# Where VectorE adds the next turn's rows in two attention stages of a four-layer kernel

## The chip, the cores and the metric

The kernel runs on one core of a Trainium2 chip, as one program. The metric is device time in microseconds, here the median of three runs. A core has TensorE (PE in the rows; its weight loads PEld), VectorE (DVE), ScalarE (ACT), GpSimd (POOL) and SyncE (SP), each with a program of its own that it runs in order; semaphores tie them together. DMA queues move data between HBM and SBUF.

## The reference

Four layers, each an attention and a mixture-of-experts feed-forward, with a residual sum after each; x is 32 x 128 x 128 in f32. What matters here is the second attention and the fourth, and the sum ahead of each:

```python
x = x + _L0_ffn_ref(_layernorm(x), ...)
x = x + _L1_xattn_ref(_layernorm(x), ctx_1024, ...)
...
x = x + _L2_ffn_ref(_layernorm(x), ...)
x = x + _L3_xattn_ref(_layernorm(x), ctx_1024, ctx_1024, mask, ...)
```

A feed-forward gives each token two experts' rows; the token's x becomes x + w0·row0 + w1·row1. The second attention is linear: q is a softmax over 8 channels of each of 16 heads, multiplied with a small matrix per batch entry, normed, added to q and projected. The fourth is an ordinary masked softmax attention with one head.

## The kernel before, in words

Tokens are held in SBUF as 32 tiles of 128 x 128, in eight groups of four. An attention runs in two turns (`TURNS` = 2); a turn works on four groups side by side, called streams w = 0 to 3 (`W` = 4), each with two PSUM banks of its own.

In both stages the program of VectorE for turn i is:

- `head_norms` (L481): scales, then the normed rows of all four streams (L477); TensorE waits for them.
- A `weave` (L94) of generators. It calls each once per round, in order, until all have ended. Four are the streams' `body`, the fifth is `next_rows` (L487), which prepares the rows of turn i + 1.
- `tail_norms`, the aggregates, scales and norms for the router of the next feed-forward; then `tail_dve` (L555), the top experts from the router's logits.

In the second attention `body` (L1679) has three steps: the maxima of the query heads and the subtraction (L1673, L1674), the head step (L1686 to L1693), and the sum into x with its statistics (L1696, L460). In the fourth, `body` (L2481) has: the maxima of the scores (L2484, L2485), the reciprocals (L2488), the final sum into x (L2493).

For one stream `next_rows` waits until the loaded pair of expert rows is there, adds it into x with eight instructions (`combine`, L523), and takes statistics and aggregates (L460, L456): four of each. These sixteen instructions are called a block here; block w is that of stream w. The tuple `rounds` says how many blocks go into each call of the generator. With (2, 2), blocks 0 and 1 follow the first step of all four bodies, blocks 2 and 3 the second step. Only turn 0 has a next turn, so turn 1 runs without blocks.

The pairs are loaded by SP at the start of the stage, in eight transfers of 512 KB (`load_pairs`, L1562), four for turn 0 and four for turn 1. In the fourth attention GpSimd scatters the rows to their experts (L2408) as soon as VectorE knows the places, and SP loads expert weights behind the pairs.

Of the kernel before, what the change touches and what calls it, by code (L numbers as in the profile page):

```python
# [4 lines left out]


# [1 line left out]

# [85 lines left out]
def weave(bodies):  # L94


    bodies = list(bodies)
    while bodies:
        bodies = [b for b in bodies if next(b, "end") != "end"]
# [14 lines left out]
def build(nc, A, out):  # L114
    with ExitStack() as top:
# [70 lines left out]
        W = 4  # L186
# [300 lines left out]
        def next_rows(dve, ch, i, st, here, rounds):  # L487

            if i < TURNS:
                w = 0  # L490
                for n in rounds:
                    for _ in range(n):
                        here(i, w)
                        known(dve, ch, st, w, x_tile(i * W + w))
                        w += 1
                    yield
                assert w == W
# [1133 lines left out]
        def attention_1(layer_before):  # L1631
            assert layer_before in SCATTERED
            with ExitStack() as ph:
                SS = streams(pe=["turn_u", "q", "turn_q", "out", "turn_o", "proj"],
                             act=["u_turned", "q_exp", "q_turned", "o_turned"],
                             dve=["u_normed", "q_less", "o"])
# [23 lines left out]
                @block.vector  # L1660
                def _(dve):
                    ch = Chain(dve)

                    def heads(ap):
                        return ap.rearrange("p (h c) -> p h c", c=8)

                    def wide(ap):
                        return ap.unsqueeze(2).to_broadcast([P, G * 16, 8])

                    def less_max(t, name, rows):  # L1670

                        red = t["red"][:, 0, :].rearrange("p (j h) -> p j h", h=16)
                        ch.link(dve.tensor_reduce(red, rows, AX.X, ALU.max))  # L1673
                        return dve.tensor_tensor(t[name].rearrange("p (j h c) -> p j h c", h=16, c=8), rows, red.unsqueeze(3).to_broadcast([P, G, 16, 8]), ALU.subtract)  # L1674

                    def here(i, w):
                        combine_stream(dve, ch, i, w, layer_before)

                    def body(w, i, S, t):  # L1679
                        g, A_, B_ = i * W + w, t["A"], t["B"]  # L1680
                        dve.wait_ge(S.pe.sem, S.PE.at(i, "q"))
                        less_max(t, "q", A_.rearrange("p (j h c) -> p j h c", h=16, c=8)).then_inc(S.dve.sem, S.DVE.tick("q_less"))
                        yield
                        dve.wait_ge(S.pe.sem, S.PE.at(i, "out"))
                        three = A_[:, 0:3 * KX].rearrange("p (j c) -> p j c", c=KX)
                        dve.reciprocal(t["dinv"][:, 0:3, :], three[:, :, P:KX])  # L1686
                        ch.link(dve.reciprocal(t["dinv"][:, 3, :], B_[:, P:KX]))
                        o, q = flat(t["u"][:, :, :]), t["q"].rearrange("p (j h c) -> p j h c", h=16, c=8)
                        dve.tensor_tensor(t["u"][:, 0:3, :].rearrange("p j (h c) -> p j h c", c=8), three[:, :, 0:P].rearrange("p j (h c) -> p j h c", c=8),
                                          t["dinv"][:, 0:3, 0:16].unsqueeze(3).to_broadcast([P, 3, 16, 8]), ALU.mult)  # L1690
                        dve.tensor_tensor(heads(t["u"][:, 3, :]), heads(B_[:, 0:P]), t["dinv"][:, 3, 0:16].unsqueeze(2).to_broadcast([P, 16, 8]), ALU.mult)
                        ch.link(dve.tensor_tensor(q, q, t["dinv"][:, :, 16:32].unsqueeze(3).to_broadcast([P, G, 16, 8]), ALU.mult))
                        dve.tensor_tensor(o, o, t["q"], ALU.add).then_inc(S.dve.sem, S.DVE.tick("o"))  # L1693
                        yield
                        dve.wait_ge(S.pe.sem, S.PE.at(i, "proj"))
                        ch.link(dve.tensor_tensor(flat(group(X, g)), flat(group(X, g)), A_[:, :], ALU.add))  # L1696
                        stats_of(dve, st_tail, w, x_tile(g))
                        yield
                    for _ in next_rows(dve, ch, 0, st, here, (W,)):
                        pass  # L1700
                    ch.link()
                    for i in range(TURNS):
                        head_norms(dve, ch, i, SS, st, T)
                        weave([body(w, i, SS[w], T[w]) for w in range(W)] + [next_rows(dve, ch, i + 1, st, here, (2, 2))])
                        ch.link()
                        tail_norms(dve, ch, i, SS, st_tail, T, taken=True)
                        weave(tail_dve(dve, ch, i * W + w, i, SS[w], T[w]["tl"], T[w]["A"]) for w in range(W))

                @block.scalar
# [655 lines left out]
        def attention_3(layer_before):  # L2365
            SCALE = float(P) ** -0.5
            with ExitStack() as ph:
# [109 lines left out]
                @block.vector  # L2477
                def _(dve):
                    ch = Chain(dve)

                    def body(w, i, S, t):  # L2481
                        g, A_ = i * W + w, t["A"]
                        dve.wait_ge(S.pe.sem, S.PE.at(i, "scores"))
                        ch.link(dve.tensor_reduce(t["nmax"][:, :], A_[:, :].rearrange("p (j l) -> p j l", j=G), AX.X, ALU.max, negate=True))  # L2484
                        dve.tensor_scalar(t["nmax"][:, :], t["nmax"][:, :], SCALE, None, ALU.mult).then_inc(S.dve.sem, S.DVE.tick("max"))  # L2485
                        yield
                        dve.wait_ge(S.act.sem, S.ACT.at(i, "exp"))
                        ch.link(dve.reciprocal(t["rinv"][:, :], t["sums"][:, :]))  # L2488
                        yield
                        dve.wait_ge(S.pe.sem, S.PE.at(i, "mixed"))  # L2490
                        for j in range(G):
                            xt = x_tile(g)(j)
                            dve.scalar_tensor_tensor(xt, A_[:, j * P:(j + 1) * P], t["rinv"][:, j:j + 1], xt, ALU.mult, ALU.add)  # L2493
                        yield
                    ch.link(dve.tensor_scalar(region[:, :], iota8[:, :], float(REGION), None, ALU.mult))
                    dve.tensor_copy(ends[:, :], region[:, :])

                    def placed(i, w):
                        own, B_ = slice(w * G, (w + 1) * G), T[w]["B"]
                        dve.wait_ge(places_made.sem, NG + i * W + w + 1)  # L2500
                        ch.link(dve.tensor_tensor(place[:, own, :], B_[:, 0:G * E].rearrange("p (j e) -> p j e", e=E), ends[:, :].unsqueeze(1).to_broadcast([P, G, E]), ALU.add))
                        dve.tensor_tensor(ends[:, :], ends[:, :], B_[:, G * E:(G + 1) * E], ALU.add)
                        ch.link(dve.tensor_tensor(place[:, own, :], place[:, own, :], hot[:, own, :], ALU.mult))
                        ch.link(dve.tensor_reduce(spot_f[:, own], place[:, own, :], AX.X, ALU.add))
                        dve.tensor_copy(spots[:, i, own], spot_f[:, own]).then_inc(positions_made.sem, 1)

                    def here(i, w):
                        combine_stream(dve, ch, i, w, layer_before)
                    for _ in next_rows(dve, ch, 0, st, here, (W,)):
                        pass  # L2510
                    for i in range(TURNS):
                        head_norms(dve, ch, i, SS, st, T)
                        weave([body(w, i, SS[w], T[w]) for w in range(W)] + [next_rows(dve, ch, i + 1, st, here, (2, 2))])
                        ch.link()
                        tail_norms(dve, ch, i, SS, st_tail, T)
                        for w in range(W):
                            weave([tail_dve(dve, ch, i * W + w, i, SS[w], T[w]["tl"], T[w]["A"], [hot])])
                            if w:
                                placed(i, w - 1)
                        placed(i, W - 1)  # L2520
                    ch.link()
                    dve.tensor_copy(pad_at, ends[0:1, :]).then_inc(ends_known.sem, 1)
                    tile_tables(dve, ch, TILES_TOP1, ends[:, :], region[:, :], marks, scratch)
                    dve.tensor_tensor(expo, LG[:, :, :], MX[:, :, 0:1].to_broadcast([P, B, E]), ALU.subtract).then_inc(leads_made.sem, 1)
                    dve.wait_ge(leads_exp.sem, 2)
                    ch.link(dve.tensor_reduce(scratch[:, 7, 0:B], expo, AX.X, ALU.add))
                    dve.reciprocal(WT[:, 0, :], scratch[:, 7, 0:B])
# [33 lines left out]
```

## Time and profile before

| What | us |
|---|---|
| median of three runs | 1773.26 |
| lowest, highest | 1766.41, 1776.73 |
| span of the profiled execution (first to last instruction) | 1780.2 |
| TensorE busy | 1444.8 (81%) |
| VectorE busy | 1162.8 (65%) |
| ScalarE busy | 818.9 (46%) |
| GpSimd busy | 764.0 (43%) |
| mean granted clock of TensorE | 0.880 |

For the profiled execution the record gives its span alone, so its own time stands here as 1780.2 us from the first to the last instruction, with nothing known to lie around it. Busy shares are averages over stages with different limits, so the stages have to be read one by one. The second attention lies between about 380 and 530 us of the span, the fourth between 1518 and 1650.

### The profile page before, as it was taken

To read this page: it belongs to the slowest core of one execution; us is meant where nothing else is said; L and a number is where in the kernel's file an instruction comes from. 1 tells how busy PE (TensorE), PEld (TensorE's weight loads), DVE (VectorE), ACT (ScalarE), POOL (GpSimd) and SP (SyncE) were. 2 spreads that over 40 slices of the span, in tenths; PEclk is the share of its full clock that TensorE was granted. 3 is DMA by queue.
4 is the path that set the end of the run, shared out by engine and by line. 5 is a ranking of instruction groups with operands and counts; after the bars stand their busy time and mean duration, and the time that the engine had idled before them with its cause. 6 is when DMAs were issued, how large, how long until landed. Compare 5 with 4: busy or idle time off the path is not lost. (4 is left out here: it accounts for less than half of the span.)

```text
span 1780.2 us, 37318 instructions
## 1 busy us (share of the span) xinstructions
PE 1444.8 (81%) x10610; PEld 1313.5 (74%) x10611; DVE 1162.8 (65%) x3689; ACT 818.9 (46%) x2528; POOL 764.0 (43%) x757
## 2 busy tenths in 40 slices
PE   6686699927767489999999999999997698446494
PEld 4565499925556389999999999999996698235494
DVE  5657744448675467778787777878785565585343
ACT  4252255512212166666666666666663233314252
POOL 3137344410003454546556565647463466012442
PEclk9696899966667699999999999999998799767697
DMA  9101122230121300000000000000000232500224
GB/s 236 21 19 58 48 59 62 62 111 1 48 94 49 118 13 1 13 1 18 9 17 7 15 9 13 10 0 12 1 13 13 76 84 76 189 12 15 73 64 120
DMA packets 94154, 82.79 MB, mean 47 GB/s; under 512 B 17076, under 2 KB 81047, under 8 KB 93927
## 3 DMA queue, kind: packets, MB, share of 16 engines
q1 hardware_dynamic: 74952, 52.24, 10.6%
q0 software_dynamic: 11936, 24.55, 4.2%
q10 hardware_dynamic: 7168, 4.86, 1.0%
q8 instruction: 42, 0.69, 0.2%
q14 instruction: 56, 0.46, 0.1%
HBM read 51.93 MB, written 31.25 MB: 47 GB/s over the span
## 5 line engine op out<-in xcount | busy, mean ns | idle before, releaser
L1980 POOL TENSOR_TENSOR paired_rows<-paired_rows,rinv 128x1024 f32<-128x1024 f32 x128 | 242.3, 1893 | 288.3 <-DVE rinv L2263 284.8
L2254 DVE TENSOR_TENSOR probs_turned_lo<-psum_banks,probs_turned_hi 128x512 fp32r<-128x512 f32 x256 | 175.6, 686 | 99.7 <-ACT probs_turned_hi L2128 92.9
L2146 ACT ACTIVATE paired_rows<-psum_banks,neg_max 128x256 f32<-128x256 f32 x512 | 237.4, 490 | 0.2
L2027 PE MATMUL psum_banks<-y_turned_parts,queries_hi 128*128 128x256 f32 x1024 | 201.4, 294 | 3.0 <-DVEq L1881 3.0
L2062 PE MATMUL psum_banks<-probs_turned_hi,y_rows 128*128 128x512 f32 x512 | 191.8, 415 | 0.4 <-issue 0.4
L2128 ACT CAST probs_turned_hi<-psum_banks 128x512 fp32r<-128x512 f32 x256 | 151.1, 590 | 56.8 <-PE psum_banks L2011 54.3
L2268 DVE TENSOR_REDUCE neg_max<-psum_banks 128x4 f32<-128x1024 f32 x128 | 156.4, 1222 | 8.9 <-PE psum_banks L2027 4.7
L2027 PEld LDWEIGHTS psum_banks<-y_turned_parts,queries_hi 128*128 128x128 f32 x1024 | 159.2, 192 | 3.6 <-issue 3.6
L2011 PE MATMUL psum_banks<-ident,paired_rows 128*128 128x128 f32 x1024 | 154.7, 274 | 7.7 <-DVEq L1881 4.4
L2128 ACT CAST queries_hi<-psum_banks 128x512 fp32r<-128x512 f32 x128 | 75.0, 586 | 174.7 <-PE psum_banks L2050 168.3
L2027 PE MATMUL psum_banks<-y_turned_parts,queries_lo 128*128 128x256 f32 x512 | 145.3, 284 | 0.0
L2074 PEld LDWEIGHTS psum_banks<-expert_w_a,paired_rows 128*128 128x128 f32 x1024 | 133.8, 191 | 11.9 <-DVE paired_rows L2278 0.7
L2050 PE MATMUL psum_banks<-expert_w_b,expert_w_a 128*128 (+1 forms) x1024 | 139.0, 279 | 2.8 <-ACT tail_turned L2118 1.8
L2074 PE MATMUL psum_banks<-expert_w_a,paired_rows 128*128 128x128 f32 x1024 | 134.8, 274 | 0.5 <-issue 0.5
L2050 PEld LDWEIGHTS psum_banks<-expert_w_b,expert_w_a 128*128 128x128 f32 x1024 | 126.5, 194 | 6.3 <-ACT tail_turned L2118 3.2
L2011 PEld LDWEIGHTS psum_banks<-ident,paired_rows 128*128 128x128 f32 x1024 | 119.8, 142 | 10.3 <-DVEq L1881 5.1
L2254 DVE TENSOR_TENSOR queries_lo<-psum_banks,queries_hi 128x512 fp32r<-128x512 f32 x128 | 88.5, 692 | 42.3 <-ACT queries_hi L2128 35.8
L1410 POOL DMA_INDIRECT expert_rows<-expert_rows_sb,tile_rows x71 | 70.6, 994 | 103.1 <-DVE expert_rows_sb L1497 103.1
L1470 ACT ACTIVATE hidden<-psum_banks,tile_w 128x128 f32<-128x128 f32 x284 | 81.2, 368 | 71.0 <-PE psum_banks L1436 71.0
L2146 ACT ACTIVATION_READ_ACCUMULATOR paired_rows<-psum_banks,neg_max 128x1 f32 x512 | 113.4, 221 | 0.0
L2062 PEld LDWEIGHTS psum_banks<-probs_turned_hi,y_rows 128*128 128x128 f32 x512 | 96.4, 188 | 17.1 <-issue 0.5
L2062 PE MATMUL psum_banks<-probs_turned_lo,y_rows 128*128 128x512 f32 x256 | 100.8, 394 | 0.0
(691 smaller groups left out, 3330.1 us busy)
## 6 DMA issues: line engine op xcount, KB each, us to landing
paired_rows<-expert_rows SPq DMA_DIRECT2D x16, 512.0 KB, 6.0
tile_rows<-rows_by_expert SPq DMA_DIRECT2D x110, 64.5 KB
tile_rows<-rows_by_expert_first SPq DMA_DIRECT2D x71, 64.5 KB
expert_w_b<-in_L_ffn_w_dram SPq DMA_DIRECT2D x2, 2048.0 KB, 12.7
tile_rows<-expert_rows SPq DMA_DIRECT2D x8, 512.0 KB, 3.6
x_rows<-in_x_dram SPq DMA_DIRECT2D x8, 256.0 KB, 5.3
normed_rows_dram<-paired_rows SPq DMA_DIRECT2D x1, 2048.0 KB, 8.7
expert_w_a<-in_L_ffn_gate_up_w_dram SPq DMA_DIRECT2D x1, 2048.0 KB, 9.5
```

The lines of the kernel that those rows point to most:

```text
L1410: pool.indirect_dma_start(ys, bass.IndirectOffsetOnAxis(ap=to, axis=0), yo[:, i % SLOTS, :], None).then_inc(expert_out[i % SLOTS].sem, 16)
L1470: ins = act.activation(hidT[:, s % 2, c * P:(c + 1) * P], hidden_bank(s, c // 2)[:, c % 2 * P:(c % 2 + 1) * P], ACT.Gelu, bias=w1[:, s % 4 ...
L1980: ins = pool.tensor_tensor(probs[:, p, :, :], probs[:, p, :, :], rinv[:, p, :].unsqueeze(2).to_broadcast([P, 4, 256]), ALU.mult)
L2011: ins = pe.transpose(bank[T_BANK][:, h * P:(h + 1) * P], probs[:, par, h, c * P:(c + 1) * P], ident[:, :])
L2027: ins = pe.matmul(bank[S_BANKS[par] + h // 2][:, (h % 2) * 256:(h % 2 + 1) * 256], queries[q][:, h, :], yparts[:, 2 * s2 + y, :], start=(k ...
L2050: ins = pe.matmul(bank[Q_BANK][:, h * P:(h + 1) * P], wqk[:, 4 * u3 + h, :], flat(KVT[:, bass.ds(b3, 1), P:2 * P]), start=True, stop=True)
L2062: ins = pe.matmul(bank[Z_BANK][:, :], yrows[:, 2 * s1 + y, k * P:(k + 1) * P], probsT[p][:, (u + 1) % 2, k, :], start=(k == 0 and n == 0), ...
L2074: ins = pe.matmul(bank[Y_BANK][:, 0:P], mixed[:, par, h, :], wvo[:, 4 * u0 + h, :], start=(u0 == 0 and h == 0), stop=(u0 == 3 and h == 3), ...
L2128: ins = act.copy(dst, bank[bank_][:, :])
L2146: ins = act.activation(probs[:, par, h, :], bank[S_BANKS[par] + h // 2][:, (h % 2) * 256:(h % 2 + 1) * 256], ACT.Exp, bias=nmax[:, par, h: ...
L2254: ins = dve.tensor_tensor(lo, bank[bank_][:, :], hi.bitcast(F32), ALU.subtract)
L2268: ins = dve.tensor_reduce(nmax[:, par, :], ps[:, S_BANKS[par]:S_BANKS[par] + 2, :].rearrange("p r (h k) -> p (r h) k", k=256), AX.X, ALU.m ...
```

## The change

In both stages the generator `next_rows` is made before the weave and called once ahead of it. In the second attention its rounds become (1, 1, 1, 0, 1): block 0 comes between `head_norms` and the maxima, block 1 behind the maxima, block 2 behind the head step, none behind the sums, and block 3 between `tail_norms` and `tail_dve`. `itertools.islice(ahead, 3)` lets the weave take just three calls. In the fourth attention the rounds stay (2, 2): blocks 0 and 1 come between `head_norms` and the maxima, blocks 2 and 3 behind the maxima.

```diff
@@ second attention
                     for i in range(TURNS):
                         head_norms(dve, ch, i, SS, st, T)
-                        weave([body(w, i, SS[w], T[w]) for w in range(W)] + [next_rows(dve, ch, i + 1, st, here, (2, 2))])
+                        ahead = next_rows(dve, ch, i + 1, st, here, (1, 1, 1, 0, 1))
+                        next(ahead, None)
+                        weave([body(w, i, SS[w], T[w]) for w in range(W)] + [itertools.islice(ahead, 3)])
                         ch.link()
                         tail_norms(dve, ch, i, SS, st_tail, T, taken=True)
+                        for _ in ahead:
+                            pass
                         weave(tail_dve(dve, ch, i * W + w, i, SS[w], T[w]["tl"], T[w]["A"]) for w in range(W))
@@ fourth attention
                     for i in range(TURNS):
                         head_norms(dve, ch, i, SS, st, T)
-                        weave([body(w, i, SS[w], T[w]) for w in range(W)] + [next_rows(dve, ch, i + 1, st, here, (2, 2))])
+                        ahead = next_rows(dve, ch, i + 1, st, here, (2, 2))
+                        next(ahead, None)
+                        weave([body(w, i, SS[w], T[w]) for w in range(W)] + [ahead])
                         ch.link()
                         tail_norms(dve, ch, i, SS, st_tail, T)
```

## Rows read from the trace of the kernel before

**Rows 1.** Windows: us, busy of PE, PEld, DVE, ACT, POOL; clock, DMA, GB/s.

```profile
380.00:530.00 150.00, 89.68 (x432) 71.44 (x432) 108.22 (x474) 28.92 (x57) 0.34 (x1) 0.61 0.19 64
...
640.00:1480.00 840.00, 808.57 (x6241) 765.34 (x6240) 629.79 (x1447) 496.89 (x1545) 473.53 (x436) 0.98 0.06 18
...
1518.00:1650.00 132.00, 71.13 (x392) 50.65 (x392) 91.22 (x506) 41.79 (x121) 20.34 (x21) 0.71 0.23 74
```

**Rows 2.** Timeline of VectorE, second attention, turn 0: start, us, instruction, idle before it.

```profile
408.19 0.69 DVE L1673 TENSOR_REDUCE head_sums<-psum_banks 128x64 f32<-128x512 f32 x1 [3.75 <-PE psum_banks L1743]
...
417.19 2.35 DVE L523 SCALAR_TENSOR_TENSOR x_rows<-paired_rows,mix_weights,x_rows 128x128 f32<-128x128 f32 x8
...
420.85 2.32 DVE L523 SCALAR_TENSOR_TENSOR x_rows<-paired_rows,mix_weights,x_rows 128x128 f32<-128x128 f32 x8
...
424.48 0.73 DVE L1686 RECIPROCAL d_inv<-psum_banks 128x96 f32<-128x96 f32 x1
...
436.76 2.35 DVE L523 SCALAR_TENSOR_TENSOR x_rows<-paired_rows,mix_weights,x_rows 128x128 f32<-128x128 f32 x8
...
444.06 0.65 DVE L1696 TENSOR_TENSOR x_rows<-x_rows,psum_banks 128x512 f32<-128x512 f32 x1
...
450.33 1.17 DVE L456 BATCH_NORM_AGGREGATE mean_var___<-norm_stats___ 128x2 f32<-128x6 f32 x16
...
459.71 0.19 DVE L557 COPY tail_logits____<-psum_banks 128x32 f32<-128x32 f32 x1 [2.44 <-PE psum_banks L588]
```

**Rows 3.** Timeline of VectorE, second attention, turn 1, which has no blocks.

```profile
488.01 0.76 DVE L1686 RECIPROCAL d_inv<-psum_banks 128x96 f32<-128x96 f32 x1 [2.58 <-PE psum_banks L1762]
...
504.14 0.69 DVE L1696 TENSOR_TENSOR x_rows<-x_rows,psum_banks 128x512 f32<-128x512 f32 x1 [3.75 <-PE psum_banks L1743]
...
506.66 0.69 DVE L1696 TENSOR_TENSOR x_rows<-x_rows,psum_banks 128x512 f32<-128x512 f32 x1 [0.89 <-PE psum_banks L1743]
...
511.44 1.17 DVE L456 BATCH_NORM_AGGREGATE mean_var___<-norm_stats___ 128x2 f32<-128x6 f32 x16
...
521.58 0.19 DVE L557 COPY tail_logits____<-psum_banks 128x32 f32<-128x32 f32 x1 [3.21 <-PE psum_banks L588]
```

**Rows 4.** Timeline of VectorE, fourth attention, turn 0.

```profile
1550.62 0.69 DVE L2484 TENSOR_REDUCE neg_max<-psum_banks 128x4 f32<-128x512 f32 x1 [7.65 <-PE psum_banks L2427]
...
1554.15 2.35 DVE L523 SCALAR_TENSOR_TENSOR x_rows<-paired_rows,mix_weights,x_rows 128x128 f32<-128x128 f32 x8
...
1562.42 2.35 DVE L523 SCALAR_TENSOR_TENSOR x_rows<-paired_rows,mix_weights,x_rows 128x128 f32<-128x128 f32 x8
...
1569.72 1.09 DVE L2493 SCALAR_TENSOR_TENSOR x_rows<-psum_banks,rinv,x_rows 128x128 f32<-128x128 f32 x4
1570.73 1.12 DVE L2493 SCALAR_TENSOR_TENSOR x_rows<-psum_banks,rinv_,x_rows 128x128 f32<-128x128 f32 x4
```

**Rows 5.** Timeline of VectorE, fourth attention, turn 1, which has no blocks.

```profile
1614.45 0.17 DVE L2485 TENSOR_SCALAR neg_max___<-neg_max___ 128x4 f32<-128x4 f32 x1
...
1619.44 1.13 DVE L2493 SCALAR_TENSOR_TENSOR x_rows<-psum_banks,rinv,x_rows 128x128 f32<-128x128 f32 x4 [1.56 <-PE psum_banks L2435]
```

**Rows 6.** Timelines of TensorE (second and fourth attention, turn 0) and GpSimd.

```profile
438.48 2.08 PE L1743 MATMUL psum_banks<-wsmall,u_turned 128*128 128x128 f32 x8
...
445.66 1.16 PE L1743 MATMUL psum_banks<-wsmall,u_turned___ 128*128 128x128 f32 x8
...
1557.90 5.38 PE L2435 MATMUL psum_banks<-ctx_rows,expert_w_a 128*128 x32
...
1643.80 0.96 POOL L2408 DMA_INDIRECT rows_by_expert<-paired_rows,top_experts  x1 [32.13 <-DVE top_experts L2505]
```

**Rows 7.** Timeline of SP's issues of the pair loads, and all landings on that tile.

```profile
378.81 10.01 SPq L1562 DMA_DIRECT2D paired_rows<-expert_rows  x8
...
1518.68 8.69 SPq L1562 DMA_DIRECT2D paired_rows<-expert_rows  x8
...
DMA to landing us min/median/max: 1.6/6.2/12.2
```

More of the change, by code:

```diff
@@ L7 @@
 from contextlib import ExitStack
+import itertools
 import concourse.bass as bass
```

## The prediction

> **What bounds the kernel now.** I began with busy time by stage. In the second attention (380 to 530 us) and the fourth (1518 to 1650) no engine is full: VectorE works 108.2 of 150 and 91.2 of 132 us, TensorE 89.7 and 71.1 at a granted clock of 0.61 and 0.71, DMA moves little [rows 1]. Such a stage is bound by a chain that hops between engines, so I next read VectorE in order of time, with the idle time before each row and what ended it. VectorE runs its program in order, so the rows of the next turn (eight adds, four statistics and four aggregates for each of four streams) stand between other steps and push them back, unless they lie where VectorE would have waited anyway. Turn 1 of each attention has no next turn: it shows the same chain without them, and so how long each wait really is [rows 3, 5].
>
> One such block takes half of the way from 417.19 to 424.48, 3.645 us [rows 2]. Four make 14.58 us in each attention. In turn 0 of the second attention VectorE waits 3.75 us before the first maximum and 2.44 before the first logits, with no block in either; in the fourth it waits 7.65 us before its first maximum while four blocks stand behind the maxima [rows 2, 4]. Those waits are what can be used.
>
> **The change, part by part.** No instruction is added or removed. In the second attention blocks 0 and 3 move, 32 instructions of VectorE with their drains (blocks 1 and 2 keep their places); in the fourth all four blocks do, 64. No DMA, no SP or GpSimd instruction moves; each block takes its wait for its pair of rows along.
>
> Second attention, turn 0:
>
> (a) Block 0 goes ahead of the maxima. VectorE is free at 408.19 − 3.75 = 404.44; the block runs to 408.09. The first projection is there at 408.19 [rows 2]. Cost nothing, with 0.10 us to spare; without that cover it would be 3.65.
>
> (b) Block 1 alone now stands behind the maxima, 417.19 to 420.84. Would the products be there? In turn 1 VectorE waits 2.58 us at this point [rows 3], which gives 419.8 here. So the block decides, and the head step starts at 420.84 and not at 424.48: 3.64 earlier.
>
> (c) The head step takes 436.76 − 424.48 = 12.28 us [rows 2], to 433.12. Block 2 runs to 436.76. The projection comes 3.75 us behind the head step by turn 1 [rows 3], at 436.87. The sums thus start at 436.87 for 444.06: 7.19 earlier, and now a wait of TensorE decides.
>
> (d) The sums and statistics took 450.33 − 444.06 = 6.27 us because the projections of all streams had long been there. With the projection just in time, turn 1 shows 511.44 − 504.14 = 7.30, a wait of 0.89 in it [rows 2, 3]. I take 7.30, since the cover is gone as in turn 1: aggregates at 444.17, 6.16 earlier.
>
> (e) Scales and norms take 459.71 − 2.44 − 450.33 = 6.94 us, to 451.11; block 3 runs to 454.76. The first logits come 9.38 us (turn 0) or 10.14 (turn 1) behind the aggregates, by 453.55 or 454.31 [rows 2, 3]. The block ends last: the tail starts at 454.76 for 459.71. Gain 4.95 us. Nothing waits for block 3 before the norms of turn 1, which stand behind the tail.
>
> Bounds: 1.03 more if the projections are there in time after all (step d), so 6.0; below, turn 1's pace of logits would cost up to a microsecond in the tail and a late first maximum some tenths, so 3.9. I keep 4.95, the sum by the nearest rows.
>
> Fourth attention, turn 0:
>
> (f) Blocks 0 and 1 go ahead of the maxima: VectorE is free at 1550.62 − 7.65 = 1542.97, two blocks end at 1550.26, scores come at 1550.62 [rows 4]. Nothing exposed, 0.36 to spare; without cover 7.29.
>
> (g) Blocks 2 and 3 take the place of 0 and 1 behind the maxima. The reciprocals follow as before and end at 1562.42, where the third block used to start. The final step then starts there and not at 1569.72 [rows 4]: 7.30 earlier. Is its input there? In turn 1 it comes 1619.44 − 1614.62 = 4.82 us after the last maximum [rows 5], here at about 1559.1. TensorE's 32 products end at 1563.28 [rows 6], and VectorE reaches the fourth stream only at 1562.42 + 3 x 1.01 = 1565.5. So nothing waits. What is late next is VectorE itself: 3.3 us of blocks stay exposed. Bounds: 7.30 above, since only that much leaves the path; 6.4 below, if the wait for logits behind it grows by the 0.9 us by which it differs between turns of the second attention (2.44 and 3.21) [rows 2, 3].
>
> **Rows must have landed.** VectorE now wants turn 1's first rows at 404.44 and 1542.97. SP has issued all eight loads by 388.82 and 1527.37, and the slowest landing is 12.2 us after its issue [rows 7]: 401.0 and 1539.6. No wait.
>
> **Does the gain reach the end?** Behind both attentions each step follows on the one before: the row scatter of the fourth starts at 1643.80 after GpSimd sat idle 32 us [rows 6], so it moves with VectorE. The weights loads in these stages are issued after steps of the same chain. Nothing in the rows is tied to an absolute time. Sum: 4.95 + 7.30 = 12.25 us, 0.69% of the profiled span of 1780.2. That span is 7 us above the median of 1773.26, so the profiled execution was one of the longer ones; the two stages hold no row that would account for it, so I take the same 12.25 off the median: 1761.0.
>
> **TensorE's clock.** In this stage the granted clock is 0.61, a mix of the two levels, 1.2 and 2.4 GHz. Eight projection matmuls take 2.08 us at the low level, soon after TensorE stood idle, and 1.16 at the high one [rows 6]. The change shortens idle times of TensorE in turn 0, so the level may rise earlier or later in each burst. The blocks hide most of it: only step (d) would gain, by 1.03 us, giving 1760.0. The Trainium skill (TensorE: Matmul & The Clock Gate, HAM oscillation) says that bursts parted by waits start at the low clock each time; by that rule, which the first projection row bears out, step (d) stays at 7.30.
>
> **The rivals.** (A) Forecast, chance 0.64: 10.3 to 13.3 us by the bounds, 1761.0; with the scatter of medians (the three runs shown span 10.3 us) 1756 to 1767.
> (B) One attention keeps its time, 0.20: in the second the chain is tight at (a) and (c), by 0.10 and 0.11 us, and a delay of the first maximum could run through; then the time is 1773.26 − 7.30 = 1766.0, within 0.5% of before. For it: spare of a tenth only. Against: the second to fourth maximum each have a wait of their own ahead, which absorbs some.
> (C) The moved adds change nothing, 0.08: the weave could put the blocks in the same places, or another engine ends last, so 1773. Against: VectorE's idle rows name TensorE's outputs, and these wait for VectorE in turn.
> (D) The gain passes, but TensorE gets its clock at other points in later stages. The stretch 640 to 1480 holds TensorE busy for 808.6 of 840 us at 0.98 [rows 1]. If its granted clock fell to 0.966, 1.5% of 840 us would be 12.3 us and eat the gain; from 0.955 on (2.5%, 21 us) the kernel is slower by over 0.5%, about 1782. For it: the stretch is entered 5 us earlier, in another phase. Against: at this busy share the rows show 0.98 and no sign of a fall. 0.04.
> (E) The rows of turn 1 come late, against the landing above: VectorE would hold the first maximum, and each microsecond of lateness costs one. 0.04, about 1768.
>
> **How the numbers follow.** What this kernel's measurement can tell from no change is about 0.5%, 8.9 us. Of case A some 0.05 falls short of it by scatter, and 0.03 of B fall beyond it: 0.64 - 0.05 + 0.03 = 0.62 faster. Slower is D, 0.04, and 0.01 of C by scatter: 0.05. The rest is within: 0.33. The range has to take in A and B with the scatter, and leaves C, D and some of E out: 1754 to 1770.
>
> **What would show it.** The profile after should have: block 0 at 404.4 and the first maximum of the second attention still 3.75 us behind the norms; three further blocks, behind the maxima, the head step and the norms; sums with a wait of TensorE before them; the tail some 50.3 us behind the norms of turn 0 (before 55.3). In the fourth: two blocks in the former 7.65 us wait, the final step 19.4 us behind the norms (before 26.7). A DMA wait before a moved block, a maximum later than 408.5, or a clock under 0.97 between the two attentions would prove it wrong.

## The result, and the profile after

The changed kernel takes 1772.48 us, median of nine runs (1762.07 to 1778.21). The kernel before, run nine times with it, takes 1781.72 (1766.41 to 1788.1). The ratio is 0.9943 with a 95% interval of 0.992 to 0.9965: 10.2 us faster (the two medians stand 9.24 apart). That is 0.57%, just beyond the 0.5% named as what can be told from no change. The forecast ratio, 1761.0 / 1773.26 = 0.9931, lies inside the interval; the forecast time, 1761.0 with a range up to 1770, does not hold 1772.48. Three executions of 2523 to 4906 us, in the two kernels with block 0 back and with two blocks ahead, are in no ratio below.

Timeline of VectorE in the second attention of the changed kernel, turn 0 (start, us, instruction, idle before it and what ended it). Lines stand one to five higher than before:

```profile
408.76 1.11 DVE L478 TENSOR_SCALAR u_rows___<-x_rows,mean_var__,rstd__ 128x128 f32<-128x128 f32 x4
409.79 1.14 DVE L524 SCALAR_TENSOR_TENSOR x_rows<-paired_rows,mix_weights,x_rows 128x128 f32<-128x128 f32 x4
411.36 1.14 DVE L524 SCALAR_TENSOR_TENSOR x_rows<-paired_rows,mix_weights,x_rows 128x128 f32<-128x128 f32 x4 [0.44 <-issue]
...
413.82 0.66 DVE L1674 TENSOR_REDUCE head_sums<-psum_banks 128x64 f32<-128x512 f32 x1
...
416.16 0.69 DVE L1674 TENSOR_REDUCE head_sums_<-psum_banks 128x64 f32<-128x512 f32 x1 [0.92 <-PE psum_banks L1748]
...
422.62 2.35 DVE L524 SCALAR_TENSOR_TENSOR x_rows<-paired_rows,mix_weights,x_rows 128x128 f32<-128x128 f32 x8
...
426.28 0.72 DVE L1687 RECIPROCAL d_inv<-psum_banks 128x96 f32<-128x96 f32 x1
...
438.55 2.35 DVE L524 SCALAR_TENSOR_TENSOR x_rows<-paired_rows,mix_weights,x_rows 128x128 f32<-128x128 f32 x8
...
442.38 0.69 DVE L1697 TENSOR_TENSOR x_rows<-x_rows,psum_banks 128x512 f32<-128x512 f32 x1
...
444.92 0.69 DVE L1697 TENSOR_TENSOR x_rows<-x_rows,psum_banks 128x512 f32<-128x512 f32 x1 [0.91 <-PE psum_banks L1748]
...
447.33 0.69 DVE L1697 TENSOR_TENSOR x_rows<-x_rows,psum_banks 128x512 f32<-128x512 f32 x1 [0.77 <-PE psum_banks L1748]
...
450.57 1.26 DVE L457 BATCH_NORM_AGGREGATE mean_var___<-norm_stats___ 128x2 f32<-128x6 f32 x16
...
457.52 2.34 DVE L524 SCALAR_TENSOR_TENSOR x_rows<-paired_rows,mix_weights,x_rows 128x128 f32<-128x128 f32 x8
...
461.18 0.16 DVE L558 COPY tail_logits____<-psum_banks 128x32 f32<-128x32 f32 x1
```

The stage begins 5.43 us later in this profile than in that of before, which has nothing to do with the change; take 5.43 off to compare with [rows 2]. Block 0 stands in the former wait of 3.75 us. It needs 4.03 us and not 3.64, as VectorE had no next instruction for 0.44 us in its middle, so the first maximum is 0.2 us late, where the forecast had 0.1 to spare; the second still waits 0.92 for TensorE, and block 1 starts at 417.19 on the old clock, to the hundredth where it stood. Head step at 420.85 (forecast 420.84), block 2, sums at 436.95 (436.87). Then the sums have two waits for TensorE, 0.91 and 0.77, where the forecast had one of 0.89: they take 8.19 us, not 7.30. Block 3 stands behind the norms and the logits wait for it: tail at 455.75 (forecast 454.76, before 459.71).

The fourth attention, turn 0, same view:

```profile
1541.39 2.36 DVE L524 SCALAR_TENSOR_TENSOR x_rows<-paired_rows,mix_weights,x_rows 128x128 f32<-128x128 f32 x8
...
1549.16 0.69 DVE L2489 TENSOR_REDUCE neg_max<-psum_banks 128x4 f32<-128x512 f32 x1 [0.38 <-PE psum_banks L2432]
...
1552.68 2.35 DVE L524 SCALAR_TENSOR_TENSOR x_rows<-paired_rows,mix_weights,x_rows 128x128 f32<-128x128 f32 x8
...
1560.95 1.12 DVE L2498 SCALAR_TENSOR_TENSOR x_rows<-psum_banks,rinv,x_rows 128x128 f32<-128x128 f32 x4
...
1577.72 0.19 DVE L558 COPY tail_logits________<-psum_banks 128x32 f32<-128x32 f32 x1 [2.06 <-PE psum_banks L589]
```

Two blocks lie in the wait and leave 0.38 us of it (forecast 0.36). The final step has no wait before it and starts 1560.95 − 1541.39 = 19.56 us behind the norms (forecast 19.4, before 26.7).

From here on a stage's length is the time from the first scale row (`newton<-mean_var`) of turn 0 to that of turn 1. It was 68.16 us in the second and 60.44 in the fourth attention, and is 64.80 and 53.46: 3.36 and 6.98 shorter, 10.34 together. Windows of the changed kernel over the two stages and the long stretch between them (columns as in [rows 1]) show the granted clock of that stretch unmoved:

```profile
380.00:535.00 155.00, 93.45 (x442) 75.48 (x443) 110.91 (x485) 30.82 (x59) 2.24 (x2) 0.60 0.20 66
640.00:1480.00 840.00, 808.64 (x6247) 766.00 (x6247) 629.68 (x1448) 496.08 (x1543) 473.30 (x435) 0.98 0.07 18
1517.00:1641.00 124.00, 70.27 (x392) 50.13 (x392) 91.00 (x505) 41.84 (x121) 20.27 (x21) 0.73 0.25 79
```

The spans of the two profiles differ by less than the stages, 1780.2 and 1772.4: the second attention begins 5.4 us later in the profile of the changed kernel, the way from it to the fourth takes 3.6 us less (1066.79 for 1070.38), and what follows the fourth 0.7 more. All three lie outside the change; where this scatter comes from is taken up below.

### The profile page after: what moved, and what is told of

It reads as the page before. It is cut to its first block and busy times, and to the rows that moved or that the text cites. A ratio compares the mean times of both kernels' runs of the same rounds, so it can differ in the third digit from the quotient of the medians.

```text
span 1772.4 us, 37318 instructions
## 1 busy us (share of the span) xinstructions
PE 1439.5 (81%) x10610; PEld 1307.8 (74%) x10611; DVE 1164.0 (66%) x3689; ACT 819.1 (46%) x2528; POOL 764.3 (43%) x757
## 3 DMA queue, kind: packets, MB, share of 16 engines
q1 hardware_dynamic: 74952, 52.24, 11.2%
```

## The experiments

Open after the result: whether the two stage gains reach the end, what a block costs in each place, and why the absolute time missed by 11 us where the ratio fits. Ratios are to the kernel before, run on the same chip beside each group.

**The changed kernel, once more.** No edit.

> The changed kernel once more, beside before on the same chip, to separate the gain from the scatter of the time. Theory 1 (the stage gains of the profile after, 3.4 us in the second attention and 7.0 in the fourth, reach the end and nothing else changes): 10.3 us faster, ratio 0.9942. Rival (the forecast sum of 12.25 holds on average and the first profile of after was one with slow projections in the second attention): ratio 0.9931, and in this profile the sums of the second attention, turn 0, take 7.3 us and not 8.2. Rival (part of the gain is lost behind the stages): ratio above 0.996.

Measured: 0.9919 (0.9895 to 0.9943), 1763.4 us beside 1777.91. Stages 61.85 and 53.25. The sums took 8.30 us, so the forecast's 7.30 is not what turn 0 shows. This ratio alone would fit the forecast sum; the next repeats decide.

**One attention at a time.** The other one has its line of before:

```diff
-                        ahead = next_rows(dve, ch, i + 1, st, here, (2, 2))
-                        next(ahead, None)
-                        weave([body(w, i, SS[w], T[w]) for w in range(W)] + [ahead])
+                        weave([body(w, i, SS[w], T[w]) for w in range(W)] + [next_rows(dve, ch, i + 1, st, here, (2, 2))])
```

> Only the second attention has the new places; the fourth is as before. Theory 1: the time from the norms of turn 0 to those of turn 1 falls from 68.15 to 63.3 - 65 us, 3.4 us faster in all, ratio 0.9981. Forecast's sum: 4.95 us, 0.9972. Rival (a late first maximum runs through): no gain, 1.000.

> Only the fourth attention has the new places; the second is as before. Theory 1: 7.0 us faster, ratio 0.9961, and with the run above the two gains add up to that of both. Rival (the two interfere through the point at which TensorE's clock rises): the sum of the two differs from both together by over 3 us.

Measured: second alone 0.9973 (0.9951 to 0.9996), fourth alone 0.998 (0.9966 to 0.9994). The fourth's stage is 53.12, its full 7 us shorter, yet the time fell by 3.6 only. And the second attention of the kernel with only the fourth changed, whose code there is that of before, took 63.27 us and not 68.16. Its rows on TensorE, turn 0:

```profile
404.06 0.98 PE L621 MATMUL psum_banks<-ident,u_rows___ 128*128 128x128 f32 x4
404.97 0.38 PE L1739 MATMUL psum_banks<-bias_rows,ones 3*128 3x512 bf16 x1
405.28 1.16 PE L1744 MATMUL psum_banks<-wsmall,u_turned 128*128 128x128 f32 x8
...
409.50 1.16 PE L1744 MATMUL psum_banks<-wsmall,u_turned___ 128*128 128x128 f32 x8
```

Eight projection matmuls take 1.16 us, the high level of the clock (2.4 GHz), from the first stream on. In the profile of before and in the first one of the changed kernel they take 2.08, the low level (1.2 GHz), for all four. Same code in this stage, 4.9 us apart. So I ran a null and the parts again.

**Before against itself, and the parts again.**

> The kernel before, run as if it were the changed one: it shows how far two identical programs come out apart, and gives a second profile of before. If the scatter comes from the points at which TensorE's clock rises: ratio 1.000 within 0.002, and in this profile turn 0 of the second attention (68.16 us in the first profile of before, 63.27 in that of the kernel with only the fourth attention changed, whose second attention is the same) may take either value, with the clock in its first projections.

> The changed kernel a third time. Theory 1 (stage gains of 3.4 and 7.0 us pass to the end): 0.9942. Theory 2 (the two places work together, so that the whole is worth more than the parts, by a higher share of fast clock): near the 0.9919 measured last, and below the sum of the two parts by 0.003.

> Only the second attention changed, again. Theory 1: 0.9972 to 0.9981. Theory 2: the same, with times in two groups by TensorE's mean clock, about 10 us apart (0.887 and more, 0.882 and less).

> Only the fourth attention changed, again. Theory 1: the stage gain of 7.0 us passes on, 0.9961; the 0.998 measured last is then scatter. Theory 2 (half of the gain is lost behind the stage or by the clock): 0.998 again, with the stage still 7 us shorter in the profile.

Measured: the null 0.9998 (0.9977 to 1.0019). The changed kernel 0.9943 (0.9923 to 0.9964), second alone 0.9976 (0.9952 to 1.0001), fourth alone 0.9968 (0.9944 to 0.9992). Now the parts, 0.24% and 0.32%, add up to the whole, 0.57%. In the first group they made 0.47% for a whole of 0.81%. Theory 2, that the whole is worth more than its parts, did not come back; but each of these intervals is some two tenths of a percent wide to either side, so a difference of that size is not excluded, and only the stages show that each part passes on alone. The null's profile has turn 0 at the low clock again:

```profile
406.95 2.08 PE L1743 MATMUL psum_banks<-wsmall,u_turned 128*128 128x128 f32 x8
```

And yet its stage is 69.88 us and not 68.16. The 1.7 us come from the tail, where the level of the clock differs too. The router's matmuls of stream 0, turn 0, in the first profile of before, in the null and in the first of the changed kernel:

```profile
458.57 1.10 PE L588 MATMUL psum_banks<-router,u_turned 128*128 128x8 f32 x8
```

```profile
459.42 1.88 PE L588 MATMUL psum_banks<-router,u_turned 128*128 128x8 f32 x8
```

```profile
458.90 1.88 PE L589 MATMUL psum_banks<-router,u_turned 128*128 128x8 f32 x8
```

With the tail at the low level, before waits 3.21 us for the first logits and not 2.44, and takes 8.17 us and not 7.19 from the first logits to turn 1's first scale row. So a stage has to be compared with one that ran at the same level in both places.

**Is it the clock? TensorE kept busy ahead of the second attention.** In the changed kernel:

```diff
+                    pe.wait_ge(pairs_here[0].sem, pairs_here[0].value + 16)
+                    for _ in range(50):
+                        pe.matmul(bank[7][:, 0:P], ident[:, :], ident[:, :], start=True, stop=True)
                     for i in range(TURNS):
                         weave(body(w, i, SS[w], T[w]) for w in range(W))
```

> The changed kernel, with 50 matmuls of the identity with itself added on TensorE ahead of turn 0 of the second attention, from the landing of the first pair of rows on, where TensorE otherwise waits 32 us. Nobody reads them. If the point at which TensorE's clock rises makes the scatter: the first projections always run at the high level (1.16 and not 2.08 us for eight), the time from the norms of turn 0 to those of turn 1 is 60 to 62 us and not 64.9, the kernel is 1 to 4 us faster than the changed one (ratio to before 0.991 to 0.993), and the scatter of its times is smaller. If the scatter has another cause: no difference, 0.9935. If they run past the arrival of the normed rows: slower by the overhang.

Measured: 0.9936 (0.991 to 0.9961), stage 64.76: no effect there. The windows (us, busy of PE, granted clock, DMA share, GB/s) say why; the added matmuls ended at 396.64 and the rows came at 401.30:

```profile
389.00:391.00 2.00, 2.00 (x20) 1.00 1.10 348
395.00:397.00 2.00, 1.64 (x15) 1.00 0.00 0
397.00:399.00 2.00, 0.00 (x0) 1.00 0.00 0
399.00:401.00 2.00, 0.00 (x0) 0.85 0.00 0
401.00:403.00 2.00, 1.70 (x7) 0.50 0.00 0
```

The filling had raised the clock, and TensorE stood idle until it was back at the low level. So the same with 70 matmuls, on the changed kernel and on that of before:

> As the run with 50 matmuls, with 70: by the 12.81 us that 100 instructions took there, 140 take some 17 us from the landing of the first pair and end about half a microsecond before the first normed rows, where the last ones ended 4.66 us before and the clock was back at the low level. Theory (the clock's level in the first projections decides 3 to 5 us of the second attention): eight projection matmuls take 1.16 us in turn 0, norms of turn 0 to norms of turn 1 take 60 to 62 us for 64.9, ratio 0.991 to 0.993. Rival (the level makes no difference, since other work on VectorE decides then): 64 us and 0.9935.

> The kernel before with the same 70 matmuls. Theory: second attention 63.2 us for 68.2 to 69.9 from norms to norms, ratio to before 0.997 to 0.998. If so, the gain of the moved blocks there is 63.2 less 60 to 62, which is 1 to 3 us at the high clock, and 3.3 to 5 at the low. Rival: no gain, 1.000.

> The changed kernel once more beside these. From the four stage gains read so far (3.3 to 5.0 us in the second attention, 6.8 to 7.0 in the fourth): 10.3 to 12 us, ratio 0.9933 to 0.9942.

Measured: with 70, the changed kernel 0.9918 (0.9885 to 0.9951), that of before 0.999 (0.9968 to 1.0011), the changed one without filling 0.9944 (0.9917 to 0.9971). TensorE in the changed kernel with the filling, and VectorE's sums there:

```profile
382.10 18.04 PE L1779 MATMUL psum_banks<-ident 128*128 128x128 f32 x140 [13.87 <-DMA paired_rows<-expert_rows]
...
403.55 1.16 PE L1748 MATMUL psum_banks<-wsmall,u_turned 128*128 128x128 f32 x8
...
434.26 0.69 DVE L1697 TENSOR_TENSOR x_rows<-x_rows,psum_banks 128x512 f32<-128x512 f32 x1 [0.91 <-PE psum_banks L1748]
...
436.80 0.69 DVE L1697 TENSOR_TENSOR x_rows<-x_rows,psum_banks 128x512 f32<-128x512 f32 x1 [0.91 <-PE psum_banks L1748]
...
439.34 0.69 DVE L1697 TENSOR_TENSOR x_rows<-x_rows,psum_banks 128x512 f32<-128x512 f32 x1 [0.91 <-PE psum_banks L1748]
```

The first projections are at the high level, and the stage is 62.58 us (64.7 to 64.9 without, at the low level); in the kernel before it is 65.18 (69.88 with the first projections low and the tail low as here). The level of the clock there does lengthen and shorten the stage. But the later projections of the same turn are low throughout, and now all three sums wait for them, 9.33 us in all: part of what the first burst gives, the second takes back, and from the first scale row of turn 1 to that of its tail the same kernel takes 47.81 us, where it took 45.7 to 45.8. Expected was 63.2 for before; its tail ran at the low level. Over the whole kernel the filling is not shown to pay: 0.9918 and 0.9944 have intervals that overlap, and so have 0.999 and 1.

Stage lengths of all profiles, in us, with the level of the clock in the first projections and in the router's matmuls (tail) of turn 0 of the second attention. The last four rows belong to the kernels below:

| kernel | first projections | tail | second attention | fourth attention |
|---|---|---|---|---|
| before | low | high | 68.16 | 60.44 |
| before, null | low | low | 69.88 | 60.32 |
| before, 70 matmuls | high | low | 65.18 | 60.43 |
| fourth only, two runs | high | high | 63.27, 63.16 (as before) | 53.12, 52.94 |
| second only | high | high | 59.85 | 59.89 (as before) |
| second only, again | low | low | 64.84 | 60.50 (as before) |
| changed: first, 2nd and 3rd repeat | low | low | 64.80, 64.93, 64.71 | 53.46, 53.52, 53.84 |
| changed: 1st repeat | high | low | 61.85 | 53.25 |
| changed, 50 matmuls | low | low | 64.76 | 53.51 |
| changed, 70 matmuls | high | low | 62.58 | 53.13 |
| second, block 0 back | low | low | 68.28 | 60.42 (as before) |
| second, two ahead | high | low | 65.50 | 60.56 (as before) |
| fourth, four ahead | low | high | 68.24 (as before) | 60.99 |
| changed, one in the fourth's tail | high | low | 61.84 | 53.91 |

Like with like, the moved blocks save 5.1 us in the second attention with both low (69.88 and a mean of 64.81), 3.4 with both high (63.2 and 59.85) and 3.3 with the tail alone low (65.18, filled, and 61.85). With the tail alone high no profile of the changed stage exists.

**A block back, a block more, in the second attention.** Only this attention is changed, the rounds are

```diff
-                        ahead = next_rows(dve, ch, i + 1, st, here, (1, 1, 1, 0, 1))
+                        ahead = next_rows(dve, ch, i + 1, st, here, (0, 2, 1, 0, 1))
```

and, in the other kernel, (2, 0, 1, 0, 1).

> Only the second attention changed, with block 0 back behind the maxima beside block 1, and only block 3 moved to the place behind the norms. By the forecast's steps: head step 3.64 later than with all moves, block 2 and 3 as there; stage 3.6 us longer than in the kernel with the second attention changed, at the same clock in the first projections: 68.5 for 64.9 us, or 63.4 for 59.9. That leaves nearly nothing of the gain: ratio 0.999 to 1.001. Rival (a late first maximum costs as much as block 0 saves): stage no longer than there.

> Only the second attention changed, with blocks 0 and 1 ahead of the maxima, none behind them, block 2 behind the head step and block 3 behind the norms. The wait ahead of the maxima is 3.75 us at the low clock, so 3.5 us stick out and move the first maximum; the later maxima then find their projections there (their waits of 1.08, 0.72 and 1.08 go), so the last is 0.7 us later, and the products of the head step are late by 2.6. Theory: stage about as long as with one block ahead at the low clock (64 to 66 us), 1 to 3 us longer at the high clock. Rival (each microsecond of a late first maximum is lost): 3.5 us longer.

Measured: block 0 back, 0.9977 (0.9951 to 1.0004), stage 68.28 at the low clock. Against 64.84 for the second attention changed, that is 3.44 us for block 0; forecast step (b) had 3.64. The ratio says less, its interval holds both. Two blocks ahead, 0.9985 (0.9965 to 1.0006), stage 65.50 at the high clock. VectorE there:

```profile
411.08 0.66 DVE L1674 TENSOR_REDUCE head_sums<-psum_banks 128x64 f32<-128x512 f32 x1
...
420.60 0.76 DVE L1687 RECIPROCAL d_inv<-psum_banks 128x96 f32<-128x96 f32 x1 [4.00 <-PE psum_banks L1767]
```

With the same levels in projections and tail, one block ahead gives 61.85 and 61.84, so the second costs 3.65 us, more than the 1 to 3 expected and all of the block, as the rival said: the first maximum is late, nothing waits between the maxima that could absorb it, and behind them VectorE waits 4.00 us for the products. One block is what this wait holds.

**Four ahead, and one in the tail, in the fourth attention.** With the second as before, `(2, 2)` becomes `(4,)`:

> Only the fourth attention changed, all four blocks ahead of the maxima. The wait there is 7.6 us, four blocks are 14.58: the maxima come 6.9 us later, and nothing stands between them and the reciprocals, so the final step comes 5 us behind the last maximum: at 1542.97 + 14.58 + 3.53 + 4.82 = 1565.9 on the clock of before, for 1569.72 before and 1562.4 with two and two. Theory (a block costs only what sticks out of its wait): stage 3.8 us faster than before, 3.2 slower than two and two, ratio about 0.998.

Measured: 0.9979 (0.9961 to 0.9997), stage 60.99. The final step starts 29.75 us behind the first scale row, 2.7 earlier than before (32.44) where 3.8 were expected, and the stage is still 0.5 us longer than before. Most of the loss is in the tail: the wait for the first logits is 2.71 us for 1.84, and from there to turn 1 it takes 13.30 for 11.50. With all else as in the changed kernel, one block moved to the tail of the fourth attention:

```diff
-                        ahead = next_rows(dve, ch, i + 1, st, here, (2, 2))
+                        ahead = next_rows(dve, ch, i + 1, st, here, (2, 1, 0, 0, 1))
                         next(ahead, None)
-                        weave([body(w, i, SS[w], T[w]) for w in range(W)] + [ahead])
+                        weave([body(w, i, SS[w], T[w]) for w in range(W)] + [itertools.islice(ahead, 3)])
                         ch.link()
                         tail_norms(dve, ch, i, SS, st_tail, T)
+                        for _ in ahead:
+                            pass
```

> As the changed kernel, but in the fourth attention block 3 stands between the norms and the tail, as in the second; blocks 0 and 1 ahead of the maxima and block 2 behind them stay. If 3.3 us of blocks stay exposed ahead of the final step of the fourth attention: that step starts up to 3.3 us earlier, when TensorE's products are there, and the wait for the logits (2.06 us) hides part of block 3, which leaves 1.6 exposed: 1.3 to 1.8 us faster than the changed kernel. Rival (TensorE's products set the end of the final step): no faster, or slower by up to 1.6.

Measured: 0.9903 (0.9883 to 0.9924), beside 0.9919 for the changed kernel of the same group, intervals overlapping. The stage does not bear a gain out: 53.91 for 53.25. The final step is 2.4 us earlier (22.64 for 25.04 behind the first scale row), the tail gives it back. The tail's matmuls on TensorE, first with the fourth only changed, then four ahead, then one in the tail:

```profile
1561.34 1.11 PE L580 MATMUL psum_banks<-ident,u_rows 128*128 128x128 f32 x4 [10.89 <-DVE u_rows L478]
...
1565.32 0.95 PE L589 MATMUL psum_banks<-router,u_turned 128*128 128x8 f32 x8
```

```profile
1575.68 1.11 PE L580 MATMUL psum_banks<-ident,u_rows 128*128 128x128 f32 x4 [8.90 <-DVE u_rows L478]
...
1581.24 1.85 PE L589 MATMUL psum_banks<-router,u_turned_ 128*128 128x8 f32 x8
```

```profile
1560.17 1.11 PE L580 MATMUL psum_banks<-ident,u_rows 128*128 128x128 f32 x4 [8.95 <-DVE u_rows L478]
...
1565.73 1.85 PE L589 MATMUL psum_banks<-router,u_turned_ 128*128 128x8 f32 x8
```

Each burst starts at the low level after an idle time. In the first it rises before the router's matmuls, in the other two it does not, and each stream's logits cost 1.7 us and not 0.9. Why it rises in one and not in the others is not shown; the idle time ahead is even the longest in the one that rises. It is no accident of one execution, though: in the other 14 profiles, with 10.8 to 18.2 us of idle time ahead, it rises before the router's matmuls too.

## Why the prediction was right and wrong

**The base, wrong.** "so I take the same 12.25 off the median: 1761.0". This step failed. The median of 1773.26 came from three runs; with nine it is 1781.72, and in the other groups that of before is 1777.91, 1776.94, 1778.82 and 1774.05. The profile had given the hint: its span of 1780.2 stood 7 us above, and I called it one of the longer executions. Its time was about 1782 (the span and the 1.7 us that lie around it in the changed kernel's run), within 0.3 us of the nine-run median. Of the miss of 11.5 us, 8.5 are the base (1781.72 for 1773.26) and 3.0 the gain (9.24 for 12.25, by the medians). The range was then built from "the scatter of medians (the three runs shown span 10.3 us)", which cannot show how far three runs lie off. In the later groups the changed kernel took 1763.4, 1766.74 and 1764.57, inside the range; so scatter between groups has a part in the miss, and had the first group come out like these, the time would have fitted by luck on the same base.

**Where the scatter comes from, not seen.** The forecast gave TensorE's clock 1.03 us in step (d) and a rival over the long stretch between the attentions. From 640 to 1480 us that stretch kept 0.98. The clock moved in the attentions: the first projections of turn 0 at the low or the high level make the stage 68 to 70 or 63 us, with the same code. Raising the clock by hand moved the stage. And it moved right behind, which the forecast did not look at. Windows of the 170 us from turn 1's first scale row of the second attention on, in the profile of before and in the first with the fourth only changed (columns as in [rows 1]):

```profile
466.90:636.90 170.00, 110.19 (x729) 96.29 (x730) 96.16 (x393) 44.31 (x109) 41.54 (x44) 0.69 0.26 81
```

```profile
461.58:631.58 170.00, 109.62 (x778) 94.59 (x779) 100.17 (x400) 49.20 (x124) 46.63 (x49) 0.75 0.26 81
```

From that row to the first scale row of the fourth attention the code is the same in all kernels here. It takes 1062.9 to 1063.3 us in the four profiles whose clock in this window is 0.75, and 1066.7 to 1070.4 in the 13 with 0.69 to 0.72. That is up to 7.5 us, more than the first projections are worth. The way from the start of the kernel to the second attention's first scale row, the same code too, takes 396.5 to 404.2 us. In the last group the twelve runs of the changed kernel go the same way: five with a mean clock of 0.889 to 0.891 took 1756.5 to 1760.9 us, four at 0.879 to 0.881 took 1770.1 to 1776.5, the three between them 1764.3 to 1768.3. That the clock makes the scatter is shown only where TensorE was filled by hand, for the first burst, some 5 us; the rest goes with the clock and is not shown.

**(a), (b), the head step: right.** Hidden as forecast at the low clock. At the high one the wait is shorter (2.47 us in the profile with only the fourth changed), block 0 sticks out, and (a) no longer costs nothing: the first maximum comes 9.65 us behind the first scale row for 8.17, and the head step is 2.4 us earlier and not 3.6 (18.99 for 21.34); the price of too much ahead is the full block, as two ahead showed.

**(d), mis-sized by 0.9.** Turn 1 has one wait in the sums because the clock had risen by its third projection. In turn 0 it rose later, and a second wait of 0.77 came: 8.19, 8.30, 8.32 and 8.12 us in four profiles of the changed kernel. The forecast took the cover of turn 1 as that of turn 0. Only where the clock rose in the second projection, in the first profile with the second only changed, did the sums keep one wait and take 7.05.

**(e), mis-sized by 0.6.** The tail started right behind block 3. From there to turn 1's first scale row it took 7.80 us for 7.19, since the logits of streams 2 and 3 came at the low clock's pace. The bound named it. With (d) the stage gain is 3.36 for 4.95, below the bound of 3.9. But the profile of before had the high level in this tail and that of the changed kernel the low one. Against the null, which was low too, the gain is 5.1: close to 4.95, but by luck: (d) cost 0.9 there as well, and the tail of the null was 1.7 us longer than the one that the sum was made from. The high level came in this tail in four of six profiles with the old places and in one of eleven with moved blocks; whether the moves cause that is not shown.

**(f), (g): right.** 6.98 for 7.30, and 7.0 over all profiles (59.9 to 60.6 against 52.9 to 53.8 us). Nothing waited in the final step, and the wait for the logits grew by 0.2. The lower bound of 6.4 rests on a wrong difference: 2.44 and 3.21 are 0.77 apart and not 0.9, which makes it 6.5; nothing hangs on it.

**Landing, passing on: right.** No DMA wait stands before a moved block. The parts of the second group add up to the whole within their intervals, and four measurements of the whole, 0.9943, 0.9919, 0.9943 and 0.9944, mean 0.9937, make 11.2 us of 1778 for 10.3 by the first profile's stages and 12.25 by the forecast.

**The rivals.** (B), a late first maximum that runs through, did not come about with one block, and did with two. (C) and (E) fell. (D) had the right cause for the scatter, the clock, in the wrong place: in the attentions and the 170 us behind the first scale row of turn 1, not in the stretch that it named, and not against the change.

## What to carry to other kernels

A turn of the same loop without the moved work shows how long each wait is, and placing work in it by that length gave the gain to within two microseconds. But take the length at both levels of TensorE's clock: a wait of 3.75 us at one was 2.5 at the other, and work fitted to a tenth of a microsecond fits at one level only. For the same reason compare two profiles of a stage only where the clock stood at the same level in each burst; here 68.16 and 69.88 us came from one kernel. And a median of three runs is no base for an absolute forecast where a profile of the same kernel stands 7 us off it.

## What the hardware showed that I had not expected

The same program ran the same four projections at 2.08 us each in some executions and 1.16 in others. With the same levels in the tail the stage around them differed by 4.9 us in the kernel before (68.16 and, in a kernel with the same code there, 63.27) and by 3.0 in the changed one (64.80 and 61.85), as much as the change moves there. TensorE kept busy until the rows came held the high level (stage 62.58 for 64.8 us), while filling that ended 4.66 us earlier was worth nothing.

Shortening an idle time of TensorE did not help its clock: with 8.90 us of idle ahead of it the tail of the fourth attention ran low throughout, with 10.89 it rose, as it did in the 14 other profiles with 10.8 to 18.2. What decides this was not found.

VectorE paused 0.44 us with no one to wait for in the middle of block 0. In the kernel before, a pause of the same length stood at a subtraction between the maxima, inside a wait. At the low level it cost nothing in either place; at the high one the first maximum starts right behind block 0 with no wait before it.
